# A four-layer hybrid network on one core: GpSimd drain, group norm, opening and landmark front rearranged

## The reference, cut to what matters

```python
def reference(x, ...):
    x = _L0_conv_ref(x, ...)      # layer norm, attention in 14x14 windows with relative positions, MLP
    x = x + _L1_conv_ref(_gn(x), ...)          # group norm, 2-D Fourier transform, two block products, back
    t = _to_tokens(x)
    t = t + _L2_attn_ref(_ln_t(t), ...)        # landmark attention + a 33-tap convolution of v
    t = t + _L2_ffn_ref(_ln_t(t), ...)         # two of eight experts for each token
    t = t + _L3_attn_ref(_ln_t(t), ...)        # full attention
    t = t + _L3_ffn_ref(_ln_t(t), ...)         # one of eight experts, with a capacity
    return _from_tokens(t, x)

def _gn(v, G=32, eps=1e-05):
    g = v.reshape(B_, H_, W_, G, C_ // G)
    m = jnp.mean(g, axis=(1, 2, 4), keepdims=True)
    s = jnp.var(g, axis=(1, 2, 4), keepdims=True)
    return ((g - m) / jnp.sqrt(s + eps)).reshape(v.shape)

# in the window attention: the relative terms that the opening's rounds make
    rel_h = jnp.einsum('bhwc,hkc->bhwk', r_q, Rh)
    rel_w = jnp.einsum('bhwc,wkc->bhwk', r_q, Rw)
    attn = (attn.reshape(-1, WS, WS, WS, WS) + rel_h[:, :, :, :, None] + rel_w[:, :, :, None, :])
# in the landmark attention
    q_l, k_l = (pool(q), pool(k))              # means over segments: the landmarks
    x_out = kernel_1 @ kernel_2_inv @ kernel_3
    v_conv = lax.conv_general_dilated(v4, Wconv, ..., feature_group_count=H)
```

## Time and profile before

| | |
|---|---|
| runs | 1154.65, 1156.06, 1159.53 us; median 1156.06 us |
| the profiled execution | 1155.44 us, span 1153.6 us, 1.84 us outside it |
| busy share of the span | PE 87%, PEld 66%, DVE 50%, ACT 36%, POOL 25% |
| mean granted clock | 0.91 |
| mean DMA rate | 79 GB/s |

### The profile page before, as it was taken

The page is one execution under the profiler, slowest core; times in us unless marked ns, Lnnn a source line. Parts: engine busy times, 40 slices in busy tenths (PEclk is TensorE's granted clock), DMA queues, the critical chain, the costliest instruction groups (busy, mean ns, idle before and its releaser), DMA issues. The chain is left out here.

```text
span 1153.6 us, 20446 instructions
## 1 busy us (share of the span) xinstructions
PE 998.3 (87%) x7506; PEld 757.4 (66%) x7507; DVE 578.9 (50%) x1394; ACT 420.4 (36%) x853; POOL 286.6 (25%) x399
## 2 busy tenths in 40 slices
PE   6896999999699699899799839999929789993996
PEld 5685778787466488688699715666727545562775
DVE  3754554653311376465575654444448477844221
ACT  3665054546232133244352101111107356651332
POOL 4464320110100112100000262555422311103242
PEclk9885899999799899899998859999969899995899
DMA  8444863330002120200003711111133433415660
GB/s 92 118 120 122 163 159 81 81 82 2 1 28 71 43 63 2 55 1 1 2 1 84 227 34 30 49 48 49 40 109 90 124 118 99 141 54 173 201 204 15
DMA packets 103318, 91.58 MB, mean 79 GB/s; under 512 B 25905, under 2 KB 95095, under 8 KB 102590
## 3 DMA queue, kind: packets, MB, share of 16 engines
q1 hardware_dynamic: 93161, 77.15, 25.3%
q0 software_dynamic: 5632, 11.07, 3.6%
q10 hardware_dynamic: 4437, 2.17, 0.7%
HBM read 64.44 MB, written 29.70 MB: 82 GB/s over the span
## 5 line engine op out<-in xcount | busy, mean ns | idle before, releaser
L1305 DVE TENSOR_REDUCE l0a_nmax<-l0a_psS 98x2 f32<-98x392 f32 x96 | 54.4, 567 | 54.8 <-PE l0a_psS L1120 50.7
L2743 ACT ACTIVATE l2e_H<-l2e_psH 128x512 f32<-128x512 f32 x40 | 21.7, 594 | 130.2 <-PE l2e_psH L2705 130.2
L895 ACT ACTIVATE l3a_PT<-l3a_psST 128x512 f32<-128x512 f32 x96 | 54.6, 595 | 32.2 <-PE l3a_psST L806 31.4
L1255 ACT ACTIVATE l0a_PT<-l0a_psST 98x392 f32<-98x392 f32 x96 | 47.2, 497 | 42.2 <-PE l0a_psST L1162 41.9
L2723 PEld LDWEIGHTS l2e_psY<-W2T,l2e_HT 128*128 128x128 f32 x320 | 51.5, 190 | 15.9 <-issue 15.8
L2666 POOL DMA_INDIRECT ys<-l2e_Y,result_of x40 | 42.0, 1049 | 72.3 <-DVE l2e_Y L2770 66.2
L2723 PE MATMUL l2e_psY<-W2T,l2e_HT 128*128 x320 | 57.3, 332 | 1.3 <-DVE l2e_Y L2770 0.8
L941 DVE TENSOR_REDUCE l3a_nmax<-l3a_psS 128x2 f32<-128x512 f32 x48 | 33.0, 687 | 25.2 <-PE l3a_psS L776 25.2
L2770 DVE COPY l2e_Y<-l2e_psY 128x384 f32<-128x384 f32 x20 | 11.2, 558 | 65.2 <-PE l2e_psY L2723 65.2
L2702 PE MATMUL l2e_psH<-W1T,l2e_XT 128*128 x80 | 41.3, 640 | 2.7 <-issue 2.0
L2661 POOL DMA_INDIRECT l2e_X<-xn,token_at x40 | 39.3, 981 | 17.1 <-issue 17.1
(11 more groups left out here) (570 smaller groups left out, 2739.6 us busy)
## 6 DMA issues: line engine op xcount, KB each, us to landing
l3w_A<-in_w SPq DMA_DIRECT2D x8, 771.0 KB, 4.6
l3w_B<-in_w SPq DMA_DIRECT2D x8, 672.0 KB, 5.4
l3a_QS<-qd SPq DMA_DIRECT2D x72, 64.0 KB, 2.2
l3a_KS<-kd SPq DMA_DIRECT2D x72, 64.0 KB, 2.3
rd<-l0q_r_p SPq DMA_DIRECT2D x24, 168.0 KB
l0a_QS<-qd SPq DMA_DIRECT2D x54, 64.0 KB
l0a_KS<-kd SPq DMA_DIRECT2D x54, 64.0 KB
W2T<-in_w2t SPq DMA_DIRECT2D x2, 1536.0 KB, 16.7
```

The source lines that it names most:

```text
L895: nc.scalar.activation(PT[n % 3][:, s, :], psST[item % 2][:, :], ACT.Exp).then_inc(exp_done, 1)
L1255: ex = nc.scalar.activation(PT[n % 3][0:WQ, s, :], psST[item % 2][0:WQ, 0:2 * W0], ACT.Exp)
L1305: mx = nc.vector.tensor_reduce(nmax[k % 2][0:WQ, 2 * j:2 * (j + 1), s], psS[item % 2][0:WQ, 0:2 * W0].rearrange("p (t k) -> p t k", t=2), ...
```

## The change

- **Drain.** `experts_any` ends its block without draining GpSimd, and the semaphores of its gathers live in the stage around it.
- **Opening.** SP no longer waits for `kbd` before the pieces of image 0; the read of `kbd` stands after image 2. The zeros and the taps of `band` are written in the window attention, after `load(4)` and `load(5)`. ACT and DVE copy out round r+1 before they split the pieces of round r. The first group's `RS` load is issued among the last rounds' writes. The six warm-up products at the window attention's start go; three like them stand at the opening's end, after the last rounding.
- **Group norm.** A class `FourierFront` holds the Fourier stage's weights and norm. Pair 0's norm, the weight loads, the clearing and the constant rows are in `l0_mlp`: the mean product before `second(2)`, the variance product before `second(3)`.
- **Landmark front.** A class `LandmarkFront` makes, in the Fourier stage's last pair, the norms and turns of images 0 and 1 and the projections of image 0; the band's rows (`toep`) are loaded and the value tiles cleared there too. The last image's statistics move the other way, into `l2_features`.
- A tile of `l2_inverse` lies in `toep`'s memory, and routing tiles are allocated earlier.

```diff
-    def block(self):
-        return self.ctx.enter_context(self.nc.Block())
+    def block(self, drained=True):
+        return self.ctx.enter_context(self.nc.Block(no_gpsimd_drain=not drained))
...
-            sp.dma_start(rows(G["band"], 0, ...), rows(consts["zeros"], ...)).then_inc(band_out, 16)
...
-            sp.wait_ge(kb_out, 16)
-            for t, piece in enumerate(K_TERM):
-                sp.dma_start(kb[t * HD:(t + 1) * HD, :], rows(G["kbd"], ...), ...).then_inc(kb_in, 16)
             for i in range(B):
...
-                if i == 0:
-                    sp.wait_ge(rev_done, 1)
-                    sp.wait_ge(band_out, 16)
-                    sp.dma_start(rows(G["band"], ...), free(backwards[:, 0:1], [0, P], [1, TAPS])).then_inc(band_out, 16)
+                if i == 2:
+                    sp.wait_ge(kb_out, 16)
+                    for t, piece in enumerate(K_TERM):
+                        sp.dma_start(kb[t * HD:(t + 1) * HD, :], rows(G["kbd"], ...), ...).then_inc(kb_in, 16)
...
                     rp.sync_each(sp, to, *piece_of(r, u))
+                    if (r, u) == (2, 0):
+                        sp.wait_ge(rp.out[0], 2 * rp.unit)
+                        sp.wait_ge(rp.out[2], 2 * rp.unit)
+                        position_rows(sp, G, RS, 0, first_in)
...
+            pe.wait_ge(rp.p1, FOURS * len(rounds))
+            for c in range(3):
+                nc.tensor.matmul(psR[:, :], G["ident"][0:CH, :], QF[:, 0, c * 2 * T:(c + 1) * 2 * T], start=True, stop=True)
...
+            relative_out(*rounds[0])
+            for r, a, axis in rounds:
+                if r + 1 < len(rounds):
+                    relative_out(*rounds[r + 1])
...
+                if k == ring:
+                    sp.dma_start(rows(G["band"], ...), rows(G["consts"]["zeros"], ...)).then_inc(band_out, 16)
+                if k == ring + 1:
+                    sp.wait_ge(band_out, 16)
+                    sp.dma_start(rows(G["band"], ...), free(G["backwards"][:, 0:1], [0, P], [1, TAPS])).then_inc(band_out, 16)
...
-            for c in range(6):
-                nc.tensor.matmul(psS[0][:, :], G["ident"][0:CH, :], G["QF"][:, 0, ...], start=True, stop=True)
...
+                if p == NP - 2:
+                    pe.wait_ge(xT_done, 2 * NP)
+                    gn.mean(pe, psT[0], 0)
+                if p == NP - 1:
+                    gn.variance(pe, psT[1], 0)
                 second(p)
...
                 if p + 1 < NP:
-                    mean(p + 1)
+                    gn.mean(pe, psM, p + 1)
+                else:
+                    lf.turn(pe, 0, psM)
+                    lf.turn(pe, 1, psV)
...
-        block = st.block()
+        block = st.block(drained=False)
```

More of the change, by code:

```diff
@@ L529, in _, with relative_out @@
                 seconds(i)
-            for r, a, axis in rounds:
+            def relative_out(r, a, axis):
                 if r >= 2:
@@ L1648, in backward @@
                 mm.then_inc(y_mm, 1)
-            mean(0)
-            variance(0)
             for p in range(NP):
@@ L1659, in _ @@
                 if p + 1 < NP:
-                    variance(p + 1)
+                    gn.variance(pe, psV, p + 1)
+                else:
+                    early.finish(pe)
+                    pe.wait_ge(lf.xT_done, 1)
+                    lf.project_queries(psM, 0)
                 second(2 * p)
@@ L1710, in _ @@
                 if p + 1 < NP:
-                    root(p + 1)
+                    gn.root(act, p + 1)
+            lf.turned_in(act, 1, psV)
+            lf.queries(act, 0, psM)
+            lf.keys(act, 0, psV)
         @block.vector
@@ L1825, in _ @@
                 if p + 1 < NP:
-                    scale(p + 1)
-                    norm(p + 1)
+                    gn.scale(dve, p + 1)
+                    gn.norm(dve, p + 1, (f_mm, lambda i: 2 * i - 2), (xs_done, lambda i: i - 1))
+                else:
+                    dve.wait_ge(lf.cleared, 2)
+                    lf.values(dve, 0, psB[1][1])
                 residual(2 * p)
@@ L1886, in _ @@
         def _(pool):
-            for u in range(2):
-                nc.gpsimd.memset(VZ[u][:], 0.0).then_inc(cleared, 1)
+            lf.stats.gpsimd(nc, pool, B - 1, (B - 1) % 2)
             for i in range(B):
@@ L1984, in landmarks @@
                 mm.then_inc(k3_mm, 1)
-            for c in range(-2, B + 1):
+            for c in range(B + 1):
                 queries = lambda: turn_queries(c - 1) if has(c - 1) else None
@@ L2003, in projected @@
             def projected(i):
-                u = i % 2
                 if i >= 2:
                     act.wait_ge(l3_mm, i - 1)
-                for ps, dst, b0, mm_done, done in ((psQ, QT, 0, q_mm, q_done), (psK, KT, 2, k_mm, k_done)):
-                    act.wait_ge(mm_done, i + 1)
-                    for a in range(2):
-                        ev = nc.scalar.activation(dst[u][:, a, :], ps[0:CH, a * T:(a + 1) * T], ACT.Identity, bias=qkb[:, b0 + a:b0 + a + 1])
-                    ev.then_inc(done, 1)
+                lf.queries(act, i, psQ)
+                lf.keys(act, i, psK)
             def exps(i):
@@ L2113, in kept @@
                 nc.vector.tensor_copy(K2L[:, 2 * i:2 * i + 2, :], ps3[0:CH, 2 * CH:2 * CH + 2 * LM].rearrange("p (a m) -> p a m", a=2)).then_inc(k3_done, 1)
-            norm(0)
-            norm(1)
-            nc.vector.tensor_scalar(hms[:, :], hm[:, :], 1.0 / (SEG * HD ** 0.5), None, ALU.mult).then_inc(cleared, 1)
-            dve.wait_ge(cleared, 3)
-            for c in range(-1, B + 1):
+            dve.wait_ge(lf.cleared, 3)
+            means(0)
+            lf.norm(dve, 2)
+            lf.stats.vector(nc, dve, B - 1, (B - 1) % 2)
+            for c in range(B + 1):
                 if has(c - 1):
@@ L2613, in slots_of_pairs, with experts_any @@
         slot(pairs // RING - 1, s, lambda ahead: s + ahead < RING)
-def experts_any(nc, G, transfers, rows_out):
+def experts_any(nc, G, transfers, rows_in, rows_out):
     with Stage(nc, "l2e") as st:
@@ L3296, in build @@
         net.window_attention()
-        net.window_mlp()
-        net.fourier()
-        net.landmark_attention()
+        net.routing()
+        with Stage(nc, "l2g") as beyond:
+            lf = LandmarkFront(beyond, net.G)
+            with Stage(nc, "l1g") as across:
+                gn = FourierFront(across, net.G)
+                net.window_mlp(gn)
+                net.fourier(gn, lf)
+            net.landmark_attention(lf)
         with Stage(nc, "l2y") as between:
-            rows_out = [between.sem(f"rows_out{r}") for r in range(RING)]
-            net.two_experts(rows_out)
+            rows_in, rows_out = ([between.sem(f"{name}{r}") for r in range(RING)] for name in ("rows_in", "rows_out"))
+            net.two_experts(rows_in, rows_out)
             with Stage(nc, "l3f") as across:
```

472 lines of the change are left out of this document (272 added, 200 removed).

## The result

The changed kernel takes 1162.53 us (median of 9 executions, 1159.21 to 1182.9), the kernel before, beside it on the same chip, 1155.81 us (9 executions, 1153.94 to 1159.53). The ratio is 1.0045, 95% interval 1.0027 to 1.0062: 0.45% slower, where 2.2% faster was forecast, and above the range of 1119 to 1140. The profiled execution took 1161.34 us, span 1159.5, mean granted clock 0.888 (before: 1153.6, 0.913).

The account below looks back on a forecast made before the run. PE, busy 87% of the span, was taken as the bound, with time only where it idles or runs at 1.2 GHz; -5.7-9.8-7.2-6.3+8.0-4.5 = -25.5 from 1155.44 gave 1129.9 us, range 1119 to 1140.

Parts of the forecast that it names:

- Window attention's start: -4.5 us: Window attention: without the warm-up products item 12 starts 10.4 to 11.4 us in; -4.5 us, bounds -0.8 and -8.
- Cold starts: Rival: each new stage start runs at 1.2 GHz (`forward`, first projection, first scores, rounds); 1140 us, chance 0.13.
- Drain, -5.7: End of `experts_any`: SP's next load starts at about 845.2 instead of 850.96; -5.7 us, bounds nothing and 6.2.
- The rival in which it does not do what it says: Rival at the drain: POOL works on its scatters until just before 850.96 by itself; 1135.7 us, chance 0.07.
- Group norm -9.8: Start of the Fourier stage: norm moved into the MLP, `forward` follows the barrier at the high clock; -9.8 us.
- landmark front -7.2: Start of the landmark stage: projection of image 1 comes first behind the barrier; -7.2 us, bounds 5.5 and 8.5.
- Opening, images, -6.3: Opening's image loop: without SP's wait for `kbd`, ACT's 6.26 us wait goes; -6.3 us, bounds 3.5 and 7.8.
- Pieces behind `kbd`: Rival in the opening: image 0's pieces queue behind `kbd`'s 2-byte elements, losing 2.8 of 6.3 us; 1133 us, chance 0.10.
- Opening, rounds, +8.0: Opening's rounds: copying a round ahead delays DVE's first rest and the last pieces; +8.0 us, bounds +1.5 and +11.
- Light rounds: Rival: the opening's rounds run at the high clock, +1.5 us instead of +8; 1123.5 us, chance 0.17.
- Band zeros and taps, 0: Writes moved behind `load(4)` and `load(5)` in the window attention: no cost, up to 3 us if not.
- the slower case by the zeros: Rival in the window attention: the zeros' write takes 32 us and holds `load(5)`'s rows and PE; 1158 us, chance 0.03.

Follow-up runs that it names:

- old front: Changed kernel with the opening and window attention of the kernel before, leaving drain, group norm and landmark front: 1135.26 us, ratio 0.9808.
- six back, rounds in the old order: Changed kernel with six warm-up products back at the window attention's start and each round copied out right before its own pieces: 1128.9 us, ratio 0.9753.
- drain alone: Kernel before with only the drain of `experts_any` left out: 1152.66 us, ratio 0.9954.
- six products back: Changed kernel with the six warm-up products back at the window attention's start, three staying at the opening's end: 1134.6 us, ratio 0.9805.
- the same without lookahead: Changed kernel, six products at the opening's end, one rounding earlier, weight loads spread behind `load(4)` to `load(7)`, rounds in old order: 1152.32 us, ratio 0.9907.
- weight loads later: Changed kernel, six products at the opening's end, 16 early weight loads issued four at a time behind `load(4)` to `load(7)`: 1149.32 to 1179.15 us.
- six at the opening's end: Changed kernel with six products instead of three at the opening's end, none in the window attention: 1161.17 us, ratio 1.0005.
- the wait filled: Changed kernel, six products at the opening's end, weight loads spread behind later groups, four wide products before the second group's wait: 1129.71 us, ratio 0.9754.

## Why the prediction was wrong

**The step that failed is "Window attention's start: -4.5 us"**, and with it the size of the rival "Cold starts". Both counted the warm-up products by the time they take. From the earlier trace rows the prediction read 8.28 us of products that compute nothing, and it let the scores run at the low clock for the first 6 us only, as if any dense work would lift it. The worst bound, -0.8 (by its own numbers, 15.3 less 14.3, it is -1.0), and the rival's +3.7 let only the first twelve items run at 1.2 GHz. There the account ended, and so far it held within its bounds: item 12 came 2.2 us earlier in the stage. For the time behind item 12 it put nothing. Measured to the stage's end: +27.65. The runs showed in its place that scores alone leave the clock down for long: 86 us of them in the changed kernel, 125 us in the longest execution of the kernel before without its six products. The earlier trace rows could not tell what would have happened without the products; the prediction treated a thing that the trace shows together (dense work, and a rise) as if the one always brought the other. Another row that it had in hand spoke against that: in the earlier trace rows PE is busy for all of the 13.65 us from 76.25 on and is granted 0.50 throughout. The rival stood on the right side (its "first scores"); of its other three places the two starts ran at 2.4 GHz and the rounds did not. The prediction gave it 0.13, and priced its first scores at 3.7 us above the forecast where they came to 27.65+4.5 = 32.2. The Trainium skill, "TensorE: Matmul & The Clock Gate", section "Why this matters for your kernels", lists warming up for accurate benchmarks, and for throughput it asks that TensorE be kept busy, which is to bring the high clock. That it speaks against dropping the warm-up was thus the prediction's own reading: by that section the dense scores would have lifted the clock by themselves. Here the trace disagrees: PE was busy for 86.31 of 86.37 us at 1.2 GHz.

**Drain, -5.7**: measured -5.72 in the stretch, and 3.6 to 7.1 us alone. The reading of the earlier trace rows holds: SP's wait was for the drain. The rival in which it does not do what it says falls.

**Group norm -9.8 and landmark front -7.2**: together -16.67 against -17.0, and each by itself near its term. From the MLP's first norm to the end of pair 0's `forward` it took 96.50 us (306.26 to 402.76) and takes 87.31 (336.96 to 424.27), -9.19; from there to the projection of image 1 80.25 and 72.77, -7.48. Both starts ran at 2.4 GHz, as the forecast took it: `forward` of pair 0 took 4.09 us. Image 0's queries stand in the last pair's products and its values and keys ahead of the last `backward`, and the last residual ends at 496.57, 0.47 us ahead of the projection of image 1:

```profile
481.85 1.89 PE L1985 MATMUL l_psM<-l2g_xT,early 96*96 96x256 f32 x8
487.41 1.57 PE L1998 MATMUL l_psB<-early,l2g_xT 96*128 96x192 f32 x8
488.81 1.89 PE L1985 MATMUL l_psV<-l2g_xT,early 96*96 96x256 f32 x8
```

With the drain, the three terms measured 19.7 to 24.6 us against 22.7 ("old front").

**Opening, images, -6.3**: -7.6, close to the upper bound of 7.8, in the two profiles. Which profiles are compared matters: 69.50, 71.94 and 71.98 us with the old opening and 61.90 and 63.20 with the new one make it -6.3 to -10.1. In times, "old front" (0.9808) and "six back, rounds in the old order" (0.9753), which differ by the rest of the opening and of the window attention, lie some 6 us apart. "Pieces behind `kbd`" falls as a cost: ACT's wait is 0.82 us, and SP's queue no longer waits for `kbd` in the image loop, only for POOL:

```profile
SPq L285 <- POOL l0q_q_p L272: 26.7, 7, 8.1
SPq L285 <- POOL l0q_k_p L272: 7.6, 7, 2.7
```

Slow they were: image 0's query pieces, issued at 25.06 us, landed 7.3 us later, where the median of the eight images is 2.8 us, and `kbd`'s write took 14.5 us from its issue at 15.6, so that both were under way together until about 30. That the one held up the other is not shown, and ACT lost only 0.82 us by it: an earlier issue did bring an earlier landing (about 32.4 us; before, ACT had the write at 39.10), against what the prediction concluded from the Trainium skill, "DMA: Bandwidth & Descriptors", section "Issuing engines are not separate DMA queues". That section says only that the transfers run on the same 16 engines and interleave. The profiled execution of before was a mild one besides: ACT's wait took 7.8 and 7.5 us in "drain alone" and "old front", which have the same opening.

**Opening, rounds, +8.0**: +10.65 in the two profiles. The mechanism is the one that was walked: DVE's first rest now stands behind round 1's copies of bank 4.

```profile
78.10 0.98 DVE L350 COPY l0q_RHW<-l0q_psK 84x112 f32<-84x112 f32 x6 [4.57 <-PE l0q_psK L464]
78.99 2.35 DVE L264 TENSOR_TENSOR early<-l0q_RHW,l0q_r_p 84x1024 f32<-84x1024 f32 x2
```

The cleaner measure is the pair of kernels with the six products back, which differ in the order alone: 7.4 us in their profiles, 0.5% (6 us) in their times. The rest of the 10.65 goes with the clock and the base: here PE ran at 1.2 GHz from 67.62 us on, the condition of the upper bound of 11, and the 48.71 us of before were on the short side (51.6 and 51.4 in "drain alone" and "old front"). The 13.65 us at 1.2 GHz that the prediction read for the rounds of before were not all: from 93.32 us to their end at 103.83 they ran at 1.2 GHz again. "Light rounds" falls.

**Band zeros and taps, 0**: no stall in the window attention with the six products back, so the slower case by the zeros falls. It was the wrong mechanism for the slower side: the price of the actual one lay in the sum's own term, with a bound of the wrong sign.

**Checked against the whole**: the sum without the failed term, -5.7-9.8-7.2-6.3+8.0 = -21.0, gives 1155.44-21.0 = 1134.4 us; "six products back", which is just that change, measured 1134.6. On its own chip, where the kernel before took 1158.19, that is 23.6 us less, 19.3 to 25.9 by the ratio's interval: the sum lies inside, and the agreement to 0.2 us is luck.

## What to carry to other kernels

A warm-up product is not to be priced by the time that it takes, but by the clock of the stage behind it: before one is removed, ask which later stretch would run at 1.2 GHz, and whether that stretch's own products have ever been seen to lift the clock; a row in which PE is busy throughout at 1.2 GHz is the warning. Work that is moved earlier is only early if its data are there; what looked like idle filler can be the cover for a load, and a wait of two microseconds that it uncovered here went with 20 us and more. Order changes that fill an engine early (the lookahead) are worth walking to the last transfer: here the walk was right, and with the products back the kernel was some 6 us faster without that part.

## What the runs showed of the hardware that was not expected

- **The scores held either level of the clock for long.** Score products (bf16, 120 to 196 columns, with small f32 products between items) ran back to back at 1.2 GHz for 86, 125, 33, 48 and 61 us before the clock rose, and at 2.4 GHz for 170 to 177 us without a fall. With four or six f32 products of 512 columns it rose 4.0 to 7.0 us after the first of them, in every kernel that had them in one row; three of them, followed by an idle of 2.71 us, did not. Whether it is their type, their width or their rows isn't told apart.
- **The clock also fell without an idle.** The rounds' products (f32, up to 112 columns) begin at 61.90 us in the changed kernel; at 67.62 the clock fell, with PE busy for all of the 5.72 us between, and to their end at 99.14 us it did not come back, with PE busy for 31.52 us of these. The same form of products on `l0q_psK`, in rounds 0 and 2:

```profile
64.58 2.89 PE L464 MATMUL l0q_psK<-QF,l0q_Rbd 96*84 96x16 f32 x36
83.19 5.32 PE L464 MATMUL l0q_psK<-QF,l0q_Rbd 96*84 96x16 f32 x36
```

- **With one idle of two to four microseconds the scores lost it**: 1.92 us in "the same without lookahead", 1.96 us in "weight loads later", 3.8 us in "six at the opening's end". Idles of 0.30 and 1.32 us in the last of these, and of 0.8 us in "the wait filled", were passed without a fall. That the idle is the cause rests on one profile of each kernel and on the run that filled it.
- **Why it rises in the end isn't settled.** It came back at 207.57 us in the changed kernel, at 249.46, 199.80, 179.99 and 177.53 in others, with no wait of PE just ahead that the profile shows. The versions in which it falls spread by 28 to 30 us (1141.04 to 1171.21, 1149.92 to 1177.73, 1149.32 to 1179.15), those in which it stays up by 3 to 13 us (1122.57 to 1125.29 and 1125.69 to 1138.62 at the two ends); that fits a rise that comes sooner or later, but no profile of the same kernel at both ends was taken.
